# A two-lane decoder on one core: the halving inside silu moved into four weight tensors, and a new table for the order of the two lanes

## The chip, the core and the metric

The kernel runs on one core of a Trainium2 chip. The metric is the device time of one execution in microseconds (us), the median over several executions. The core has five instruction queues, each of which works in its own order: TensorE (PE, with its weight loads shown as PEld), VectorE (DVE), ScalarE (ACT), GpSimd (POOL) and SyncE (SP, which issues most transfers). Queues wait for each other through semaphores.

## What is computed

Four sequences of 512 rows by 128 columns pass through six sublayers, each followed by a layer norm. Only the fourth, a selective state-space recurrence, is touched by the change:

```python
x_and_res = x @ W_in
u, res = (x_and_res[..., :d_inner], x_and_res[..., d_inner:])
u = jax.nn.silu(u)
delta = jax.nn.softplus(u @ W_delta + b_delta)
Bm = u @ W_B
Cm = u @ W_C
def step(h, inp):
    d_t, B_t, C_t, u_t = inp
    dA = jnp.exp(d_t[..., None] * A)
    h = dA * h + d_t[..., None] * B_t[:, None, :] * u_t[..., None]
    y_t = jnp.einsum('bdn,bn->bd', h, C_t)
    return (h, y_t)
y = jnp.swapaxes(ys, 0, 1) + u * D_param
y = y * jax.nn.silu(res)
return y @ W_out
```

Ahead of it come a gated long convolution (hyena), a cross attention of one head (cross0) and a feed-forward layer with quantised weights (bitffn). Behind it come a cross attention of 16 heads (cross1) and a layer that weighs 1024 experts by product keys (experts).

## The kernel before

The kernel works on two sequences at a time, called lanes 0 and 1, in two passes: pass 0 does sequences 0 and 1, pass 1 does sequences 2 and 3. Everything of a lane lies in its own tiles (mem0, ps0, x0 and so on for lane 0, mem1, ps1, x1 for lane 1). Each engine's program is written once for a lane, as a generator that yields between pieces. A table of numbers, `LANE_RUNS`, has a row for each engine and says how many pieces of lane 0 to write into the queue, then how many of lane 1, and so on in turn. The order inside a lane is fixed. The table decides only how the two lanes lie between each other, but since each queue works in order, it decides who waits behind whom.

The recurrence (function `scan`) begins when DVE has written the lane's new x (L1472). PE transposes x (L712), ACT copies it (L1165), PE multiplies it by `m_in` (L866, four products of 128 x 512), and ACT takes the tanh of half of each (L1261). DVE forms (tanh + 1) times the product (L1637), which is twice silu. For the first two products, those of u, a second DVE step halves it into the tile `uu` (L1641). PE then needs both halves of `uu` for delta (L872, with `m_delta`), and for B and C (L878 and L884, with `m_bc`). ACT makes the softplus from absolute value, exponential and logarithm (L1268, L1273, L1276), and DVE adds it up (L1651, L1656) and multiplies by `uu` (L1659). Then 16 steps follow: ACT does the decay (L1291) and the input (L1310, in the first step L1299), PE transposes (L903), DVE scans (L1668), POOL multiplies by C (L1926), PE accumulates (L914). At the end DVE adds u times D (L1674) and gates with the other two products (L1678). Those last two keep their factor of two, which is taken out in L1678.

ACT has to load another function table (ACT_TABLE_LOAD) when the next function isn't in the loaded one. In the head of the recurrence tanh, the exponential and the logarithm alternate, so the order of the lanes sets how often.

In `experts` DVE weighs a tile of 128 x 1024 sums of key scores (L1844). Eight such tiles belong to a piece of 128 rows, and four pieces to a lane. The sums come from one of three engines: PE with a copy by ACT (L1087, L1165), DVE (L1827), or ACT (four groups of eight L1412). DVE also picks the best keys (L1778, L1799) and thresholds (L1802, L1804). In `cross1` a unit is eight ACT exponentials (L1368), behind two score matmuls (L1013) and a maximum by DVE (L1719, L1721).

Two semaphores matter: `p_late` is reached when the late weights, `m_delta`, `m_bc` and `m_D` among them, have been loaded, and `p_dve` counts steps of DVE in the preparation (4 of them before).

Of the kernel before, what the change touches and what calls it, by code (L numbers as in the profile page):

```python
# [72 lines left out]
def decoder(nc, x, ctx_1024, mask_BxSxS2_ik1, L0_attn_w_in, L0_attn_b_in, L0_attn_w_conv,  # L73
# [14 lines left out]
    DJ = DI // P  # L88
    NS = L1_attn_W_B.shape[1]
# [27 lines left out]
    with ExitStack() as ctx:  # L117
# [436 lines left out]
        for s in range(LANES):  # L554
            for k in range(NB):
# [10 lines left out]
            sync=("0 1 3 2 2 2 1 1 1 1 2 1 1 1 2 2 2 1 1 2 1 1 1 1 2 3 2 1 1 1 5 2 1 2 4 2 2 1 1 1 1 1 1 "  # L566
                "2 1 2 2 5 1 1 1"),
            tensor=("3 3 2 1 1 1 3 2 1 1 1 1 1 1 1 1 1 1 1 1 3 1 1 1 1 2 1 1 1 4 5 5 5 5 1 1 1 1 1 1 1 1 1 "
# [8 lines left out]
            scalar=("4 4 1 1 3 2 2 1 1 2 2 1 1 1 2 1 1 1 1 1 1 1 1 4 4 1 1 4 4 4 1 1 4 4 3 3 1 1 2 2 1 1 2 "  # L577
# [1411 lines left out]
```

## Time and profile before

| what | us |
|---|---|
| median of 3 runs (lowest 1017.96, highest 1019.2) | 1018.46 |
| the profiled execution: its time | 1017.51 |
| its span, first to last instruction | 1015.7 |
| PE busy in it | 776.3 |
| DVE busy | 759.6 |
| ACT busy | 686.5 |
| POOL busy | 317.7 |

No engine is busy for more than 76% of the span, so the sums by engine don't give the time. The kernel is a row of stages with other limits in each, and the time is read stage by stage: what an engine that is nearly always busy there has to do, and which waits it still has.

### The profile page before, as it was taken

What the parts mean: (1) busy time and instruction counts of PE and PEld (TensorE: products, weight loads), DVE (VectorE), ACT (ScalarE), POOL (GpSimd) and SP (SyncE); (2) the same over time, 40 slices, a digit from 0 to 9 for tenths busy, and PEclk for the clock granted to TensorE, in tenths of its full rate; (3) what the DMA queues carried; (4) which work ended last, traced back from release to release, by engine and by line L of the source; (5) the groups of instructions that cost most, each with busy time, mean ns of one, the idle gap of its engine ahead of it and who ended that gap; (6) DMA issues with size and microseconds to landing.
All of it is one profiled execution on the core that took longest, in us unless ns stands there. A gap on an engine that the chain in (4) does not pass through costs nothing.

```text
span 1015.7 us, 13734 instructions
## 1 busy us (share of the span) xinstructions
PE 776.3 (76%) x4486; PEld 568.2 (56%) x4488; DVE 759.6 (75%) x1635; ACT 686.5 (68%) x2061; POOL 317.7 (31%) x191
## 2 busy tenths in 40 slices
PE   1895586777978898797878468777797889889782
PEld 0584346666556555565657334666655744657561
DVE  2667857777655679999997875778766576998994
ACT  1445389995589489758534538999558859767850
POOL 3142107776466200000025210688746620000000
PEclk9987698999999899989987778799999999779997
DMA  6500012221000000010000000223100000000000
GB/s 163 157 1 1 0 47 70 87 93 43 21 1 1 1 1 1 1 37 1 1 22 1 0 1 29 86 88 95 45 19 1 1 1 0 1 1 1 1 1 21
DMA packets 28961, 29.04 MB, mean 29 GB/s; under 512 B 7268, under 2 KB 19290, under 8 KB 28890
## 3 DMA queue, kind: packets, MB, share of 16 engines
q1 hardware_dynamic: 26776, 27.19, 9.2%
q10 hardware_dynamic: 2114, 0.99, 0.4%
q8 instruction: 35, 0.57, 0.2%
q14 instruction: 36, 0.29, 0.1%
HBM read 26.33 MB, written 1.84 MB: 28 GB/s over the span
## 4 chain that ended last, share of the span: by engine, by line
DVE 36%; PE 26%; ACT 20%; POOL 7%; issue 5%; DMA 2%; POOLq 0%; DVEq 0%; ACTq 0%
DVE mem L1844 13%; ACT mem L1368 8%; DVE mem L1827 6%; POOL mem L1926 6%; ACT mem L1310 4%; ACT mem L1291 3%; PE ps L961 2%; PE ps L1134 2%; PE ps L1000 2%; PE ps L1098 2%; DVE mem L1668 2%; DVE mem L1778 2%; PE ps L1087 2%; PE ps L1036 1%; PE ps L1147 1%
## 5 line engine op out<-in xcount | busy, mean ns | idle before, releaser
L1884 POOL TENSOR_TENSOR rs<-ve,minus_half 128x4 f32<-128x4 f32 (+1 forms) x56 | 88.4, 1580 | 492.4 <-DVE ve L1465 419.6
L1926 POOL TENSOR_TENSOR mem<-mem 128x1024 f32<-128x1024 f32 x64 | 150.9, 2378 | 105.7 <-DVE mem L1668 103.6
L1668 DVE TENSOR_TENSOR_SCAN mem<-mem,ps 128x1024 f32<-128x1024 f32 x64 | 143.3, 2275 | 52.3 <-PE ps L903 52.0
L1844 DVE SCALAR_TENSOR_TENSOR mem<-mem 128x1024 f32<-128x1024 f32 x128 | 160.4, 1283 | 17.1 <-ACT mem L1165 10.4
L1412 ACT ACTIVATE mem<-mem 128x32 f32<-128x32 f32 x768 | 166.8, 313 | 7.1 <-PE ps L1134 7.1
L1134 PE MATMUL ps<-ident,mem 128*128 128x128 f32 x1024 | 140.8, 290 | 37.2 <-DVE mem L1844 35.2
L1165 ACT ACTIVATE mem<-ps 128x1024 f32<-128x1024 f32 (+6 forms) x127 | 92.9, 747 | 105.3 <-PE ps L1087 46.7
L1134 PEld LDWEIGHTS ps<-ident,mem 128*128 128x128 f32 x1024 | 120.4, 149 | 74.8 <-DVE mem L1844 52.3
L1368 ACT ACTIVATE mem<-ps,mem,rs 128x77 f32<-128x77 f32 x256 | 101.9, 449 | 21.2 <-DVE mem L1721 21.1
L903 PE MATMUL ps<-ident,mem 128*128 128x128 f32 x512 | 77.9, 307 | 47.9 <-ACT mem L1310 21.1
L1310 ACT ACTIVATE mem<-mem 128x256 f32<-128x256 f32 x240 | 100.2, 494 | 0.0
L903 PEld LDWEIGHTS ps<-ident,mem 128*128 128x128 f32 x512 | 65.0, 158 | 58.7 <-ACT mem L1310 43.5
L1087 PE MATMUL ps<-mem 64*128 64x512 f32 x160 | 83.2, 644 | 3.9 <-ACT mem L1165 3.3
L1291 ACT ACTIVATE mem<-mem,m_A 128x511 f32<-128x511 f32 x128 | 83.1, 708 | 3.3 <-DVE mem L1668 3.1
L1827 DVE TENSOR_TENSOR mem<-mem 128x1024 f32<-128x1024 f32 x64 | 77.6, 1223 | 0.1
L914 PE MATMUL ps<-ident,mem 128*128 128x128 f32 x512 | 68.6, 285 | 9.1 <-POOL mem L1926 8.9
L914 PEld LDWEIGHTS ps<-ident,mem 128*128 128x128 f32 x512 | 60.5, 148 | 14.3 <-POOL mem L1926 13.3
L1368 ACT ACTIVATION_READ_ACCUMULATOR mem<-ps,mem,rs 128x1 f32 x256 | 61.2, 239 | 0.0
L1940 POOL TENSOR_TENSOR mem<-mem 128x616 f32<-128x616 f32 x32 | 38.9, 1215 | 47.8 <-DVE mem L1740 47.8
L1013 PE MATMUL ps<-mem,xT 128*128 128x308 f32 x128 | 41.0, 444 | 12.9 <-ACT mem L1368 11.4
L1087 PEld LDWEIGHTS ps<-mem 64*128 64x128 f32 x160 | 28.3, 196 | 37.3 <-issue 31.1
L1036 PE MATMUL ps<-vw,mem 128*128 128x128 f32 (+1 forms) x320 | 45.2, 285 | 0.0
(228 smaller groups left out, 1283.4 us busy)
## 6 DMA issues: line engine op xcount, KB each, us to landing
mem<-bc_rows SPq DMA_DIRECT2D x64, 256.0 KB, 3.3
mem<-in_x_dram SPq DMA_DIRECT2D x4, 256.0 KB, 5.4
mem<-in_L_ffn_w_q_dram SPq DMA_DIRECT2D x2, 512.0 KB, 7.7
mem<-key_rows SPq DMA_DIRECT2D x2, 512.0 KB
out_dram<-x SPq DMA_DIRECT2D x4, 256.0 KB, 2.3
mem<-in_mask_BxSxS_ik_dram SPq DMA_DIRECT2D x4, 154.0 KB, 3.8
a_k<-in_L_xattn_Wk_dram SPq DMA_DIRECT2D x1, 512.0 KB, 7.6
key_rows<-mem SPq DMA_DIRECT2D x1, 512.0 KB, 8.3
```

What stands on the lines that cost most here:

```text
L903: mm = pe.transpose(ps[:, 2 + j, k * P:(k + 1) * P], DZ[s][:, n % 2, k, j * P:(j + 1) * P], ident[:])
L914: mm = pe.matmul(ps[:, k // 2, at:at + P], HC[s][:, (n - 1) % 2, j, k * P:(k + 1) * P], ident[:], start=(n == 1 and at == 0), stop=(n == N ...
L1087: mm = pe.matmul(ps[:, 2 + half, :], SIMT[s][rows, k % 2, h // 2, :], key_pick[rows, half * (NK // 2):(half + 1) * (NK // 2), :] .rearrang ...
L1134: mm = pe.matmul(ps[:, e // 4, (e % 4) * P:(e % 4 + 1) * P], WH[s][:, (k * PH + h) % WB, e * P:(e + 1) * P], ident[:], start=(h == 0 and e ...
L1291: ins = nc.scalar.activation(dA[s][:, n % 2, j, 1:S], DL[s][:, j, 1:S], ACT.Exp, scale=m_A[:, j, n:n + 1])
L1310: ins = nc.scalar.activation(DZ[s][:, n % 2, k, :], DUT[s][:, k, :], ACT.Identity, scale=BT[s][:, k, n:n + 1])
L1368: ins = nc.scalar.activation(SC[s][:, k % 2, h, :], ps[:, i // 4, i % 4 * C:(i % 4 + 1) * C], ACT.Exp, scale=RS[s][:, k * H + h:k * H + h ...
L1412: ins = nc.scalar.activation(WH[s][:, n % WB, i * NK:(i + 1) * NK], sims[:, 1, h, :], ACT.Identity, bias=sims[:, 0, h, i:i + 1])
L1668: nc.vector.tensor_tensor_scan((HS, TU)[n % 2][s][:].rearrange(flat), dA[s][:, n % 2].rearrange(flat), dbu.rearrange(flat), 0.0, ALU.mult, ...
L1827: summed[n] = own(nc.vector.tensor_tensor(WH[s][:, n % WB, :].rearrange("p (i j) -> p i j", i=NK), spread(views(k)[:, 0, h, :], 2, NK), sp ...
L1844: nc.vector.scalar_tensor_tensor(out=wh, in0=wh, scalar=TH[s][:, k % 2, h:h + 1], in1=wh, op0=ALU.is_ge, op1=ALU.mult).then_inc(G("wh_read ...
L1926: nc.gpsimd.tensor_tensor(HC[s][:, n % 2], (HS, TU)[n % 2][s][:], spread(CQ[s][:, n % 2, :], 1, DJ), ALU.mult)\
```

## The change

The step L1641 goes away: DVE writes (tanh + 1) times the product straight into `uu`, which now holds twice u. Whoever reads `uu` gets a factor that is taken out of the weights, once, in the first pass: `m_delta` times 0.5, the C part of `m_bc` times 0.5, `m_D` times 0.5, and the B part of `m_bc` times 0.25, since B multiplies delta times u and both hold the factor. These four steps stand on DVE at the start of lane 0's `bitffn` in pass 0. PE ahead of L872 and DVE ahead of L1674 now wait for the fifth step of `p_dve`. All five rows of the table are new.

```diff
         LANE_RUNS = dict(
-            sync=("0 1 3 2 2 2 1 1 1 1 2 1 1 1 2 2 2 1 1 2 1 1 1 1 2 3 2 1 1 1 5 2 1 2 4 2 2 1 1 1 1 1 1 "
+            sync=("1 1 5 2 1 2 2 2 1 1 1 1 1 1 2 2 1 1 1 1 2 2 1 3 2 1 1 1 5 2 1 2 2 1 3 1 1 1 1 1 2 2 1 "
...
                     w.next(G("silu_u", s), DJ)
+                    pe.wait_ge(p_dve, 5)
                     for m in range(DJ):
...
                     dve.wait_ge(p_late, ALL_LATE)
+                    if s == 0 and b == 0:
+                        yield 0
+                        nc.vector.tensor_scalar(m_delta[:], m_delta[:], 0.5, None, ALU.mult)
+                        nc.vector.tensor_scalar(m_bc[:, :, 0:NS], m_bc[:, :, 0:NS], 0.25, None, ALU.mult)
+                        nc.vector.tensor_scalar(m_bc[:, :, NS:2 * NS], m_bc[:, :, NS:2 * NS], 0.5, None, ALU.mult)
+                        nc.vector.tensor_scalar(m_D[:], m_D[:], 0.5, None, ALU.mult).then_inc(p_dve, 1)
                     yield 0
                     x_squares(s)
...
-                        ins = nc.vector.scalar_tensor_tensor(out=t[:, j % DJ, :], in0=t[:, j % DJ, :], scalar=1.0,
-                                                             in1=ps[:, at, :], op0=ALU.add, op1=ALU.mult)
-                        if j < DJ:
-                            w.link(ins)
-                            nc.vector.tensor_scalar(UU[s][:, j, :], t[:, j, :], 0.5, None, ALU.mult)\
-                                .then_inc(G("silu_u", s), 1)
-                        else:
-                            ins.then_inc(G("silu_r", s), 1)
+                        to = (UU if j < DJ else TR)[s][:, j % DJ, :]
+                        nc.vector.scalar_tensor_tensor(out=to, in0=t[:, j % DJ, :], scalar=1.0, in1=ps[:, at, :],
+                                                       op0=ALU.add, op1=ALU.mult)\
+                            .then_inc(G("silu_u" if j < DJ else "silu_r", s), 1)
...
                     w.next(G("y_acc", s), NS + 1)
+                    dve.wait_ge(p_dve, 5)
                     for j in range(DJ):
```

What the new table moves is shown at three places. In the changed kernel most lines stand one or two off: its L1643 is L1637 of before, L1616, L1618 and L1624 are L1611, L1613 and L1619 (the quantising and the last sum of `bitffn`), L1471 is L1472, L1260 is L1261, L1272 and L1275 are L1273 and L1276, L1846 and L1829 are L1844 and L1827, L1780 to L1806 are L1778 to L1804.

First, DVE where the recurrence starts in pass 0. Before:

```order
L1472 TENSOR_SCALAR x0<-r0,mv0,rs0 128x128 x4
L1472 TENSOR_SCALAR x1<-r1,mv1,rs1 128x128 x4
L1637 SCALAR_TENSOR_TENSOR mem0<-mem0,ps0 128x512
L1641 TENSOR_SCALAR mem0<-mem0 128x512
L1637 SCALAR_TENSOR_TENSOR mem0<-mem0,ps0 128x512
L1641 TENSOR_SCALAR mem0<-mem0 128x512
L1637 SCALAR_TENSOR_TENSOR mem0<-mem0,ps0 128x512 x2
L1637 SCALAR_TENSOR_TENSOR mem1<-mem1,ps1 128x512
```

The same place on DVE in the changed kernel:

```order
L1471 TENSOR_SCALAR x0<-r0,mv0,rs0 128x128 x4
L1616 TENSOR_SCALAR mem1<-mem1,rs1,st1 128x512
L1618 TENSOR_SCALAR mem1<-mem1 128x512
L1643 SCALAR_TENSOR_TENSOR mem0<-mem0,ps0 128x512 x4
L1624 SCALAR_TENSOR_TENSOR r1<-ps1,st1,r1 128x128 x4
L1458 BN_STATS bns1<-r1 128x6 x4
L1461 BN_AGGR mv1<-bns1 128x2 x4
L1464 TENSOR_SCALAR ve1<-mv1 128x4
L1471 TENSOR_SCALAR x1<-r1,mv1,rs1 128x128 x4
L1652 TENSOR_SCALAR mem0<-ps0,m_bdelta 128x512 x2
```

Lane 1's last sum of `bitffn` (L1619 of before, L1624) and its new x, which stood ahead of lane 0's silu, now stand behind it.

Second, ACT at the same place in pass 0. Before:

```order
L1261 ACTIVATE mem0<-ps0 128x512 x4
L1261 ACTIVATE mem1<-ps1 128x512 x4
L1268 ACTIVATE mem0<-ps0,m_bdelta 128x512 x2
L1273 ACT_TABLE_LOAD
L1273 ACTIVATE mem0<-mem0 128x1024
L1268 ACTIVATE mem1<-ps1,m_bdelta 128x512 x2
L1273 ACTIVATE mem1<-mem1 128x1024
L1276 ACT_TABLE_LOAD
L1276 ACTIVATE mem0<-mem0 128x1024
L1276 ACTIVATE mem1<-mem1 128x1024
```

The same place on ACT in the changed kernel:

```order
L1260 ACTIVATE mem0<-ps0 128x512 x4
L1267 ACTIVATE mem0<-ps0,m_bdelta 128x512 x2
L1272 ACT_TABLE_LOAD
L1272 ACTIVATE mem0<-mem0 128x1024
L1164 ACTIVATE xT1<-ps1 128x512
L1275 ACT_TABLE_LOAD
L1275 ACTIVATE mem0<-mem0 128x1024
L1164 ACTIVATE mem0<-ps0 32x512
L1164 ACTIVATE mem0<-ps0 128x64
L1260 ACT_TABLE_LOAD
L1260 ACTIVATE mem1<-ps1 128x512
```

Lane 0's tanh, exponential and logarithm now come in one go with only lane 1's copy of x between them, and lane 1's come later, with table loads of their own. Over the whole queue there are 16 loads in the place of 14, both new ones here.

Third, DVE where `experts` of lane 1 starts in pass 1. Before:

```order
L1844 SCALAR_TENSOR_TENSOR mem0<-mem0 128x1024
L1827 TENSOR_TENSOR mem0<-mem0 128x1024
L1844 SCALAR_TENSOR_TENSOR mem0<-mem0 128x1024
L1778 MAX mem1<-mem1 128x8 x16
L1790 TENSOR_TENSOR mem1<-mem1 128x8x8
L1790 TENSOR_TENSOR mem1<-mem1 128x8x12
L1790 TENSOR_TENSOR mem1<-mem1 128x8x4
L1796 TENSOR_REDUCE mem1<-mem1 128x8
L1799 MAX mem1<-mem1 128x8 x8
L1802 SCALAR_TENSOR_TENSOR mem1<-mem1 128x8
L1804 TENSOR_SCALAR mem1<-mem1 128x8
L1844 SCALAR_TENSOR_TENSOR mem1<-mem1 128x1024
```

The same place on DVE in the changed kernel, from lane 1's last key step on:

```order
L1806 TENSOR_SCALAR mem1<-mem1 128x8
L1780 MAX mem0<-mem0 128x8 x8
L1846 SCALAR_TENSOR_TENSOR mem0<-mem0 128x1024
L1829 TENSOR_TENSOR mem0<-mem0 128x1024
L1780 MAX mem0<-mem0 128x8 x8
L1846 SCALAR_TENSOR_TENSOR mem0<-mem0 128x1024
L1846 SCALAR_TENSOR_TENSOR mem1<-mem1 128x1024
```

Lane 1's first weighing stood behind two weighings of lane 0 and directly behind its own thresholds. It now stands behind six of lane 0, two of which (with other work of lane 0) are between its thresholds and it.

On ACT, lane 0's eight gelus and its first own sums (four groups of eight L1412) now follow each other in both passes with one copy of lane 0 between them. Before, in pass 1, seven copies of lane 1 and three of its gelus were mixed in, and in pass 0 six copies and two gelus. At the end of `cross1` in pass 1, lane 1 has four units of exponentials behind lane 0's last, and had two. In pass 0 it has two in both.

## Rows read from the trace of the kernel before

**Rows 1.** Part 1 of the page: busy us (share of the span) xinstructions.

```profile
PE 776.3 (76%) x4486; PEld 568.2 (56%) x4488; DVE 759.6 (75%) x1635; ACT 686.5 (68%) x2061; POOL 317.7 (31%) x191
```

**Rows 2.** Windows: from:to, length, busy us (xinstructions) by engine, TensorE clock, DMA, GB/s.

```profile
120.00:150.00 30.00, 26.44 (x96) 14.03 (x96) 15.94 (x28) 21.07 (x32) 0.48 (x1) 0.92 0.08 25
...
337.70:516.00 178.30, 155.94 (x850) 106.85 (x851) 161.80 (x399) 125.03 (x453) 5.72 (x5) 0.95 0.02 6
817.00:1000.00 183.00, 157.43 (x834) 108.42 (x834) 161.72 (x399) 123.09 (x447) 5.61 (x5) 0.92 0.00 1
```

**Rows 3.** Timeline of DVE, start of both recurrences: start, duration, instruction, idle before.

```profile
116.71 1.13 DVE L1619 SCALAR_TENSOR_TENSOR r<-ps,st,r 128x128 f32<-128x128 f32 x4
...
119.27 1.11 DVE L1472 TENSOR_SCALAR x<-r,mv,rs 128x128 f32<-128x128 f32 x4
...
125.35 0.69 DVE L1637 SCALAR_TENSOR_TENSOR mem<-mem,ps 128x512 f32<-128x512 f32 x1 [3.65 <-ACT mem L1261]
126.08 0.43 DVE L1641 TENSOR_SCALAR mem<-mem 128x512 f32<-128x512 f32 x1
126.42 0.68 DVE L1637 SCALAR_TENSOR_TENSOR mem<-mem,ps 128x512 f32<-128x512 f32 x1
...
127.48 1.30 DVE L1637 SCALAR_TENSOR_TENSOR mem<-mem,ps 128x512 f32<-128x512 f32 x2
...
151.85 2.29 DVE L1668 TENSOR_TENSOR_SCAN mem<-mem,ps 128x1024 f32<-128x1024 f32 x1 [4.68 <-PE ps L903]
...
595.59 1.12 DVE L1472 TENSOR_SCALAR x<-r,mv,rs 128x128 f32<-128x128 f32 x4 [0.44 <-POOL rs L1884]
```

**Rows 4.** Timeline of all engines, head of the recurrence in pass 1.

```profile
605.07 3.70 PE L872 MATMUL ps<-mem,m_delta 128*128 128x512 f32 x8 [0.52 <-DVE mem L1641]
...
610.80 1.06 ACT L1273 ACTIVATE mem<-mem 128x1024 f32<-128x1024 f32 x1
...
616.44 3.70 PE L872 MATMUL ps<-mem,m_delta 128*128 128x512 f32 x8 [0.42 <-DVE mem L1641]
...
616.67 1.28 ACT L1276 ACT_TABLE_LOAD   x1
...
628.32 2.29 DVE L1668 TENSOR_TENSOR_SCAN mem<-mem,ps 128x1024 f32<-128x1024 f32 x1 [5.23 <-PE ps L903]
```

**Rows 5.** Timeline of PE, head of the recurrence in pass 0.

```profile
130.62 7.03 PE L872 MATMUL ps<-mem,m_delta 128*128 128x512 f32 x16
```

**Rows 6.** Timeline of DVE, start of bitffn in pass 0.

```profile
84.16 0.43 DVE L1592 TENSOR_SCALAR mem<-mem 128x512 bf16<-128x512 f32 x1
...
90.57 2.73 DVE L1599 SCALAR_TENSOR_TENSOR mem<-ps,st,b 128x512 f32<-128x512 f32 x4 [3.77 <-remote]
```

**Rows 7.** Timeline of DVE, start of experts in pass 0 and in pass 1.

```profile
363.63 0.17 DVE L1804 TENSOR_SCALAR mem<-mem 128x8 f32<-128x8 f32 x1
369.45 1.28 DVE L1844 SCALAR_TENSOR_TENSOR mem<-mem 128x1024 f32<-128x1024 f32 x1 [5.65 <-ACT mem L1412]
...
840.58 0.17 DVE L1804 TENSOR_SCALAR mem<-mem 128x8 f32<-128x8 f32 x1
848.80 1.28 DVE L1844 SCALAR_TENSOR_TENSOR mem<-mem 128x1024 f32<-128x1024 f32 x1 [8.05 <-ACT mem L1165]
```

**Rows 8.** Timeline of ACT, start of experts in pass 1.

```profile
827.95 1.28 ACT L1421 ACT_TABLE_LOAD   x1
...
848.61 1.79 ACT L1412 ACTIVATE mem<-mem 128x32 f32<-128x32 f32 x8
```

**Rows 9.** Timeline of ACT, a table load in pass 0.

```profile
139.57 1.28 ACT L1276 ACT_TABLE_LOAD   x1
140.87 2.00 ACT L1276 ACTIVATE mem<-mem 128x1024 f32<-128x1024 f32 x2
```

**Rows 10.** Timeline of ACT: lane 1's last unit of cross1 in pass 1.

```profile
813.55 0.42 ACT L1368 ACTIVATE mem<-ps,mem,rs 128x77 f32<-128x77 f32 x1 [3.38 <-DVE mem L1721]
```

**Rows 11.** The chain that ended last (start, length, what): two units without a gap.

```profile
786.70 6.54 ACT mem L1368 x32
```

More of the change, by code:

```diff
@@ L565, in decoder @@
         LANE_RUNS = dict(
-            sync=("0 1 3 2 2 2 1 1 1 1 2 1 1 1 2 2 2 1 1 2 1 1 1 1 2 3 2 1 1 1 5 2 1 2 4 2 2 1 1 1 1 1 1 "
-                "2 1 2 2 5 1 1 1"),
-            tensor=("3 3 2 1 1 1 3 2 1 1 1 1 1 1 1 1 1 1 1 1 3 1 1 1 1 2 1 1 1 4 5 5 5 5 1 1 1 1 1 1 1 1 1 "
[8 rows of a table removed]
-            scalar=("4 4 1 1 3 2 2 1 1 2 2 1 1 1 2 1 1 1 1 1 1 1 1 4 4 1 1 4 4 4 1 1 4 4 3 3 1 1 2 2 1 1 2 "
[6 rows of a table removed]
-            vector=("3 3 2 1 2 2 2 1 1 1 1 1 1 1 1 1 1 1 1 2 4 3 1 2 2 1 2 4 1 1 1 1 4 4 1 1 1 1 1 1 1 1 2 "
[8 rows of a table removed]
-            gpsimd=("1 1 3 3 2 1 2 3 1 1 1 1 1 1 1 1 2 1 1 1 2 2 2 1 1 2 1 1 1 1 2 1 1 2 1 2 2 2 1 1 3 2 2 "
-                "1 1 2 2 1 1 2 1 1 1 1 1 1 1 2 1 1 1 1 3 3 4 4 1 1 1 1 6 2 2 1 1 1 1 1 1 2 1 2 2 2 1 2 "
-                "1 3 3 2 2 1 1 2 2 1 1 2 2 1 1 2 1 1 1 1 1 1 1 3 1"))
+            sync=("1 1 5 2 1 2 2 2 1 1 1 1 1 1 2 2 1 1 1 1 2 2 1 3 2 1 1 1 5 2 1 2 2 1 3 1 1 1 1 1 2 2 1 "
+                "1 1 1 1 5 1 2 1"),
+            tensor=("2 1 1 2 4 1 1 2 1 2 1 1 1 1 1 1 1 2 2 1 2 1 2 3 1 1 1 1 2 2 4 5 5 3 1 1 1 1 2 2 2 2 4 "
[7 rows of a table added]
+            scalar=("2 1 2 3 3 3 2 1 1 1 1 2 2 1 1 1 1 1 2 2 1 1 1 1 1 1 1 1 4 3 1 1 1 1 2 3 1 1 7 1 3 1 2 "
[6 rows of a table added]
+            vector=("3 3 3 1 1 3 2 2 1 1 5 1 1 1 1 1 1 1 1 1 2 2 1 1 1 1 2 2 1 2 1 1 4 2 2 2 1 3 1 1 2 2 1 "
[7 rows of a table added]
+            gpsimd=("1 1 3 3 4 4 1 1 1 1 4 2 1 1 1 1 1 1 2 2 1 1 1 1 2 2 1 1 2 4 3 2 2 1 1 2 2 1 1 2 2 1 1 "
+                "2 1 1 1 1 2 3 2 2 3 3 4 4 1 1 1 1 4 1 3 1 1 1 1 1 2 2 1 1 1 1 2 1 1 4 1 1 1 1 1 1 3 2 "
+                "3 1 2 2 1 3 1 1 1 2 1 1 1 5 1"))
         def in_turn(program, lane_runs):
```

42 rows, old and new, of tables (scalar, tensor, vector) are left out of this document.

## The prediction, on record before the changed kernel ran

> **What bounds the kernel now.** First the page's busy times [rows 1]: the busiest engine, PE, works for 76% of the span and DVE for 75%. So no engine's total gives the time, and a microsecond taken from DVE's total gives a microsecond only where DVE is what everything waits for. Next I cut the span into stages and read which engine is busy there [rows 2]. At the start of the recurrence in pass 0, from 120 to 150 us, DVE works 15.9 of 30 us and ACT 21.1: neither is full, and what counts is the chain from x to the first scan. In `experts` DVE works 161.8 of 178.3 us in pass 0 and 161.7 of 183.0 in pass 1, more than 88% in both. There the stage is DVE's work plus DVE's idle time, 16.5 and 21.3 us. Then I went to those idle times on DVE's timeline [rows 7]: the longest of each stage is a single wait, 5.65 us in pass 0 and 8.05 us in pass 1. Both stand in front of an L1844 right behind a lane 1 threshold step, early in the stage.
>
> **The change part by part.**
>
> *The eight halving steps that go.* Two for each lane and pass make eight L1641. From one L1637 to the next it takes 1.07 us with the halving between (125.35 to 126.42), and two without it take 1.30, so 0.65 each [rows 3]. Each removal frees 1.07 - 0.65 = 0.42 us of DVE, 3.4 us in all. On the path to the end much less of it counts. In pass 0 both lanes' L872 run in one piece with no wait shown [rows 5]: PE was still busy with L866, and it hides the halving. In pass 1 PE waits for the halving 0.52 and 0.42 us [rows 4], together 0.94. I take 0.9 us as gain; the bounds are 0 and 3.4.
>
> *The four new steps.* The nearest row for the largest, `m_delta` with 128 x 512, is a step of the same kind and width at 0.43 us [rows 6]. The other three have 2 to 32 columns, so each costs less: 4 x 0.43 = 1.7 us is the upper bound, nothing the lower. Their cover is the wait behind them: lane 0's quantised x was done at 84.16 + 0.43 = 84.6 us, and DVE then stood still 3.77 us before L1599, on PE's side of the work [rows 6]. I take nothing. If the new order has removed that cover, it costs up to 1.7 us.
>
> *The two waits for the fifth step.* PE's stands in front of L872, which ran from 130.62 us [rows 5], while lane 0's `bitffn`, where the four steps stand, was past its first step at 84 us [rows 6]; DVE's stands behind all 16 scans. Both find it done. Behind PE's wait all of the recurrence's matmuls are queued, so only a late step would cost, and none is late. I take nothing.
>
> *The table, where the recurrence starts in pass 0.* Lane 1's block from 116.71 to 119.27 stood ahead of lane 0's x [rows 3]. It now stands behind it, so lane 0's x can start 2.6 us sooner, near 116.7. From there to the first scan: in pass 1, where lane 0 already went first, it took 628.32 - 595.59 = 32.7 us, but 616.67 - (610.80 + 1.06) = 4.8 of these passed between exponential and the load for the logarithm, with lane 1's four tanh in the queue [rows 3, 4]. Those four are gone from that place in pass 0, which leaves 27.9 us and a first scan at 116.7 + 27.9 = 144.6 where it was 151.85 [rows 3]: lane 0 gains 7.2 us. Lane 1 pays: DVE reaches its last sum only after waiting for lane 0's tanh (3.65 us idle in the same situation before) and after four L1637 of 0.65, together 6.3 us. Half of each lane, (6.3 - 7.2) / 2, is -0.5 us, and that I take, because a stage that both lanes share moves with their mean. The bounds are what one lane alone would give: 7.2 us gained, or 6.3 lost with the two new table loads on top.
>
> A load starts at 139.57 and the logarithm behind it at 140.87 [rows 9], so a switch takes 1.30 us and two take 2.6. I count them as covered by ACT's 8.9 idle us between 120 and 150 [rows 2]; without that cover they cost 2.6, and the upper bound is 6.3 + 2.6 = 8.9.
>
> The Trainium skill, "ScalarE: Activation LUTs", section "What ACT_TABLE_LOAD costs", speaks against the change: it puts a switch at about 2.66 us, the load of 1283 ns and a drain of 1380 ns behind it. By that rule the two would cost 5.3 us, and if none of it were covered the time would be near 1015 instead of near 1010. The trace disagrees: the load's 1.28 us is there, the drain is not, since the logarithm starts 1.30 us after the load [rows 9].
>
> *The table, where `experts` starts.* In pass 1 lane 1's first L1844 waited 8.05 us for its sums' copy by ACT [rows 7], with lane 0's weighings queued behind it. But lane 0 couldn't have gone on either: its own ACT sums ended at 848.61 + 1.79 = 850.4, which is 22.4 us after the table load at 827.95 [rows 8]. The new ACT queue does these sums without lane 1's copies between them, and the new DVE queue puts six weighings of lane 0, not two, ahead of lane 1's first. In pass 0 the wait of 5.65 us was for these same ACT sums. If both waits vanish, 13.7 us are gained. If what is late next is as late, nothing is: next come lane 1's copies and gelus, now behind lane 0's sums on ACT. I take half, 6.9 us, the middle of bounds that no row tells apart. DVE has work for that time, so the gain is one of the whole stage.
>
> *The sum.* -0.9 - 0.5 - 6.9 = -8.3 us. The profiled execution took 1017.51 us, of which its span is 1015.7, and gives 1009.2. The median of the runs shown is 0.95 us higher, so I predict 1018.46 - 8.3, rounded to **1010 us**.
>
> **The rivals.**
>
> *More.* Both waits vanish and lane 0's lead isn't paid for by lane 1: -0.9 - 7.2 - 13.7 = -21.8 us, 996.7. For it: DVE would be near full in both `experts`, and nothing but the order kept it idle. Against it: other idle time, 16.5 - 5.65 = 10.9 us in pass 0, is spread over waits that another order can lengthen.
>
> *No change.* The waits move on instead of closing, since each queue works in order and a piece put ahead waits itself: -0.9 - 0.5 = -1.4, 1017.1. For it: pass 1 had lane 0 ahead, pass 0 had the lanes level, and yet the two `experts` took 178.3 and 183.0 us, with the same DVE work, so the order is worth only some us.
>
> *Slower.* In pass 1 lane 1 now has four units of `cross1` behind lane 0's last, not two. With both lanes at work a unit takes 6.54 / 2 = 3.3 us [rows 11]. With lane 1 alone ACT stands still 3.38 us in front of a unit [rows 10], since the next scores wait for the last exponentials. Two more such units cost 2 x 3.38 = 6.8 us in which ACT does nothing, and lane 0's gelus, which need another table, are queued behind them. If that is not made up and the waits of `experts` are only moved, it is -0.9 + 6.8 = +5.9, or 1024.4. It decides as soon as lane 1's last four units show such gaps in front of each while lane 0's first L1844 hasn't started. Against it: lane 0 is ahead by just that much, and DVE can pick its best keys meanwhile.
>
> **How the numbers follow.** The forecast (1003 to 1016) has a chance of 0.48, the larger gain 0.14, no change 0.14, slower 0.24. A measurement of this kernel tells about 0.2% from no change, 2 us here. So faster by more than that (below 1016.4) has 0.62, within it 0.14, slower 0.24. The range runs from 998 to 1025. It takes in each term's bounds taken alone: with the full 13.7 us in `experts` the sum is -15.1, 1003.4; with the 8.9 us lost at the start of the recurrence it is +1.1, 1019.6; with nothing gained in `experts`, 1017.1. It also takes in most of the larger gain and most of the slower case, and leaves out about 0.08 below and 0.10 above.
>
> **What would show it.** Right: L1637's successors 0.65 us apart and no wait of L872 for them; the first scan of lane 0 near 145 us and of lane 1 later than before; no single DVE wait over 3 us in the first 40 us of either `experts`, and DVE idle there below 10 and 14 us. Wrong: a DVE wait of the same size at another L1844; `cross1` of pass 1 longer by more than 5 us with ACT gaps of some 3.4 us in front of lane 1's last units; or a granted clock in `experts` clearly under the 0.95 and 0.92 of before [rows 2], which would be a cost of the order that I have given no price.

## The result and the profile after

The changed kernel took 1030.65 us (median of 4 executions, 1027.21 to 1032.23) where the kernel before took 1018.21 on the same chip: 1.0119 of it, 95% interval 1.0099 to 1.0138. It is 12.4 us slower, outside the predicted range of 998 to 1025. The profiled execution took 1030.98 us with a span of 1029.2.

The page's busy times of the changed kernel answer to [rows 1].

```profile
PE 772.6 (75%) x4486; PEld 566.7 (55%) x4488; DVE 764.9 (74%) x1631; ACT 690.1 (67%) x2063; POOL 318.7 (31%) x191
```

They say little of the loss: DVE is busy 5.3 us longer (with four instructions fewer), ACT 3.6 and POOL 1.0, PE less. So I went by stages again. The next rows are windows of the changed kernel at the places of [rows 2]; both `experts` run from lane 0's x to lane 0's x.

```profile
120.00:150.00 30.00, 26.07 (x114) 13.74 (x113) 15.63 (x32) 24.90 (x40) 3.37 (x2) 0.94 0.09 29
331.70:520.30 188.60, 158.04 (x827) 109.31 (x827) 159.75 (x388) 127.25 (x454) 6.18 (x5) 0.91 0.02 6
824.30:1013.40 189.10, 157.16 (x871) 109.16 (x869) 165.66 (x406) 129.85 (x479) 8.03 (x8) 0.95 0.00 1
```

In pass 0 DVE works 159.75 of 188.6 us. Its idle time there is 28.9 us, and was 16.5 [rows 2]. These windows mix length and lag, since the lanes lie further apart now. So from here on a stage runs from the middle of the two lanes' new x (L1472 of before, L1471 here) to the next such middle. DVE's timeline of the changed kernel, the four rows around `experts` of pass 0:

```profile
331.67 1.37 DVE L1471 TENSOR_SCALAR x<-ps,mv,rs 128x128 f32<-128x128 f32 x4 [1.12 <-POOL rs L1886]
...
350.03 1.36 DVE L1471 TENSOR_SCALAR x<-ps,mv,rs 128x128 f32<-128x128 f32 x4 [1.12 <-POOL rs L1886]
...
520.29 1.12 DVE L1471 TENSOR_SCALAR x<-r,mv,rs 128x128 f32<-128x128 f32 x4 [0.90 <-POOL rs L1886]
...
530.02 1.12 DVE L1471 TENSOR_SCALAR x<-r,mv,rs 128x128 f32<-128x128 f32 x4 [1.13 <-POOL rs L1886]
```

The stage is (520.29 + 530.02)/2 - (331.67 + 350.03)/2 = 184.3 us, and the lanes enter it 18.4 us apart (their lag). All stages by the same reckoning, with two kernels of the experiments (one profiled execution each):

| stage, us | before | changed | fold alone | table alone |
|---|---|---|---|---|
| until the recurrence, pass 0 | 119.9 | 119.9 | 118.6 | 123.4 |
| recurrence | 137.8 | 137.8 | 139.9 | 138.4 |
| cross1 | 85.0 | 83.2 | 84.9 | 83.2 |
| experts | 176.2 | **184.3** | 175.5 | **180.2** |
| hyena, cross0, bitffn of pass 1 | 80.2 | **85.1** | 80.0 | **85.8** |
| recurrence | 141.3 | **142.9** | 139.7 | **146.2** |
| cross1 | 82.2 | **85.1** | 82.8 | **85.9** |
| experts | 177.9 | 175.8 | 175.1 | 175.7 |

The profiled execution of the fold alone is 2.2 us below its median (given below), so the stages differ by some 2 us more in all than the medians do.

So three places lost time: `experts` of pass 0, the front of pass 1, and recurrence with `cross1` in pass 1. I had put a term on the first (as a gain), none on the second, and only a rival on the third.

**Experts.** DVE's timeline of the changed kernel, its longer waits at the start of both `experts` (answers to [rows 7]), and where lane 1's key maxima stand now (365.57):

```profile
342.54 1.59 DVE L1780 MAX8 mem<-mem 128x8 f32<-128x32 f32 x16 [3.15 <-ACT mem L1164]
...
356.35 1.28 DVE L1846 SCALAR_TENSOR_TENSOR mem<-mem 128x1024 f32<-128x1024 f32 x1
...
363.19 1.28 DVE L1846 SCALAR_TENSOR_TENSOR mem<-mem 128x1024 f32<-128x1024 f32 x1 [5.55 <-ACT mem L1411]
...
365.57 1.59 DVE L1780 MAX8 mem<-mem 128x8 f32<-128x32 f32 x16
...
398.72 1.29 DVE L1846 SCALAR_TENSOR_TENSOR mem<-mem 128x1024 f32<-128x1024 f32 x1 [3.52 <-ACT mem L1164]
...
844.59 1.29 DVE L1846 SCALAR_TENSOR_TENSOR mem<-mem 128x1024 f32<-128x1024 f32 x1 [6.74 <-ACT mem L1164]
```

DVE's timeline of the kernel before in pass 0: lane 0's third weighing, then lane 1's key maxima, which stood ahead of the wait of 5.65 us:

```profile
357.39 1.28 DVE L1844 SCALAR_TENSOR_TENSOR mem<-mem 128x1024 f32<-128x1024 f32 x1
...
360.27 1.59 DVE L1778 MAX8 mem<-mem 128x8 f32<-128x32 f32 x16 [1.59 <-ACT mem L1165]
```

ACT's timeline of the changed kernel: in pass 0 lane 0's own sums and behind them the copy of lane 1's x, in pass 1 the table load ahead of lane 0's gelus:

```profile
355.79 1.79 ACT L1411 ACTIVATE mem<-mem 128x32 f32<-128x32 f32 x8
...
357.96 5.19 ACT L1411 ACTIVATE mem<-mem 128x32 f32<-128x32 f32 x24
...
363.06 0.67 ACT L1164 ACTIVATE xT<-ps,p_norm 128x512 f32<-128x512 f32 x1
...
838.98 1.28 ACT L1420 ACT_TABLE_LOAD   x1
```

ACT does what I had read from its order: the sums stand together and end at 357.96 + 5.19 = 363.15, six us sooner than before (DVE's weighing that needs them began at 369.45 [rows 7], and begins at 363.19 now). But DVE also comes six us sooner, at 363.19 - 5.55 = 357.64 where it came at 369.45 - 5.65 = 363.80. One us of that is lane 0's third weighing, which ended at 358.67 and ends at 357.63. The other five are lane 1's key steps (360.27 to 363.80 before, with the wait of 1.59 us ahead of them): they filled that time, and now stand behind the weighing, from 365.57 on. They couldn't have filled it any more, because ACT's copy of lane 1's x now stands behind the same sums and starts at 363.06. So the wait stayed as long as it was. And new ones came: 3.15 us ahead of lane 0's key maxima, 3.52 us for a copy that ACT has queued behind lane 1's sums.

In pass 1 the wait of 8.05 us, of lane 1's first weighing for its copy, is gone. The 6.74 us at 844.59 are another wait: lane 0's first weighing waits for lane 0's first copy. ACT does lane 1's last unit of `cross1` ahead of lane 0's gelus and loads their table 838.98 - 824.34 = 14.6 us after lane 0's x, where it took 827.95 - 817.0 = 11.0 before [rows 2, 8].

**Recurrence and cross1 of pass 1.** DVE's timeline of the changed kernel at the end of lane 1's recurrence:

```profile
743.17 1.22 DVE L1710 TENSOR_REDUCE ve<-mem 128x16 f32<-128x1024 f32 x1 [2.15 <-ACT mem L1355]
...
748.14 2.29 DVE L1669 TENSOR_TENSOR_SCAN mem<-mem,ps 128x1024 f32<-128x1024 f32 x1
...
757.15 0.20 DVE L1742 RECIPROCAL mem<-mem 128x8 f32<-128x8 f32 x1 [3.36 <-ACT mem L1367]
759.63 0.80 DVE L1721 TENSOR_REDUCE mem<-ps 128x8 f32<-128x616 f32 x1 [2.27 <-PE ps L1012]
...
761.34 1.41 DVE L1676 SCALAR_TENSOR_TENSOR mem<-mem,m_D,ps 128x512 f32<-128x512 f32 x2 [0.71 <-PE ps L922]
...
770.57 1.12 DVE L1471 TENSOR_SCALAR x<-r,mv,rs 128x128 f32<-128x128 f32 x4 [0.21 <-POOL rs L1886]
```

Lane 1's last scan and its closing steps (L1676) stand behind `cross1` steps of lane 0 (L1710, L1742, L1721) that wait themselves. Lane 1's x comes 35.0 us after lane 0's (12.8 before), and then its last units of `cross1` run alone. ACT's timeline in front of three of lane 1's last five units (lane 0's last unit lies between the first and the second of these rows):

```profile
808.20 0.42 ACT L1367 ACTIVATE mem<-ps,mem,rs 128x77 f32<-128x77 f32 x1 [2.43 <-DVE mem L1723]
...
820.31 0.42 ACT L1367 ACTIVATE mem<-ps,mem,rs 128x77 f32<-128x77 f32 x1 [2.43 <-DVE mem L1723]
...
827.31 0.42 ACT L1367 ACTIVATE mem<-ps,mem,rs 128x77 f32<-128x77 f32 x1 [3.70 <-DVE mem L1723]
```

**The front of pass 1.** Two waits of PE in the changed kernel from 539.5 to 581 us (total, times, longest), which the kernel with the fold alone doesn't have in the same sublayer, `cross0`:

```profile
PE ps L736 <- DVE mem L1502: 5.2, 1, 5.2
PE ps L710 <- DVE x L1471: 4.5, 2, 4.2
```

By the middles of the lanes' new x, `cross0` took 28.6 us where it takes 24.6 with the fold alone; hyena lost 1.4 and `bitffn` none. That these two waits make the 4.0 us is argued from where they stand, not tested.

### The profile page after: what moved, and what is told of

Same layout as the page of the kernel before. It is cut to its first block, busy times and chain, and to the rows that moved or that the text cites. A ratio compares the mean times of both kernels' runs of the same rounds, so it can differ in the third digit from the quotient of the medians.

```text
span 1029.2 us, 13737 instructions
## 1 busy us (share of the span) xinstructions
PE 772.6 (75%) x4486; PEld 566.7 (55%) x4488; DVE 764.9 (74%) x1631; ACT 690.1 (67%) x2063; POOL 318.7 (31%) x191
## 4 chain that ended last, share of the span: by engine, by line
PE 26%; issue 23%; DVE 17%; ACT 16%; POOL 12%; DMA 2%; POOLq 0%; DVEq 0%; ACTq 0%
POOL mem L1928 8%; ACT mem L1367 4%; ACT mem L1411 4%; POOL rs L1886 3%; PE ps L1086 3%; DVE mem L1846 3%; DMA mem<-bc_rows 2%; ACT mem L1309 2%; PE ps L1133 2%; PE ps L960 2%; ACT mem L1290 2%; PE ps L1012 2%; PE ps L999 2%; DVE mem L1829 2%; DVE x L1471 2%
## 5 line engine op out<-in xcount | busy, mean ns | idle before, releaser
L1846 DVE SCALAR_TENSOR_TENSOR mem<-mem 128x1024 f32<-128x1024 f32 x128 | 160.5, 1278 | 23.3 <-ACT mem L1411 11.7
L1133 PEld LDWEIGHTS ps<-ident,mem 128*128 128x128 f32 x1024 | 119.7, 148 | 81.5 <-DVE mem L1846 57.0
L902 PEld LDWEIGHTS ps<-ident,mem 128*128 128x128 f32 x512 | 62.5, 153 | 51.6 <-ACT mem L1309 29.1
L1829 DVE TENSOR_TENSOR mem<-mem 128x1024 f32<-128x1024 f32 x64 | 77.4, 1218 | 0.0
L913 PEld LDWEIGHTS ps<-ident,mem 128*128 128x128 f32 x512 | 61.0, 149 | 26.2 <-POOL mem L1928 25.4
L1367 ACT ACTIVATION_READ_ACCUMULATOR mem<-ps,mem,rs 128x1 f32 x256 | 58.3, 228 | 0.0
L1012 PE MATMUL ps<-mem,xT 128*128 128x308 f32 x128 | 43.2, 463 | 13.6 <-ACT mem L1367 12.1
L1721 DVE TENSOR_REDUCE mem<-ps 128x8 f32<-128x616 f32 x32 | 25.6, 799 | 28.1 <-PE ps L1012 28.1
```

Source lines behind the costliest of these rows:

```text
L902: mm = pe.transpose(ps[:, 2 + j, k * P:(k + 1) * P], DZ[s][:, n % 2, k, j * P:(j + 1) * P], ident[:])
L913: mm = pe.matmul(ps[:, k // 2, at:at + P], HC[s][:, (n - 1) % 2, j, k * P:(k + 1) * P], ident[:], start=(n == 1 and at == 0), stop=(n == N ...
L1133: mm = pe.matmul(ps[:, e // 4, (e % 4) * P:(e % 4 + 1) * P], WH[s][:, (k * PH + h) % WB, e * P:(e + 1) * P], ident[:], start=(h == 0 and e ...
L1367: ins = nc.scalar.activation(SC[s][:, k % 2, h, :], ps[:, i // 4, i % 4 * C:(i % 4 + 1) * C], ACT.Exp, scale=RS[s][:, k * H + h:k * H + h ...
L1846: nc.vector.scalar_tensor_tensor(out=wh, in0=wh, scalar=TH[s][:, k % 2, h:h + 1], in1=wh, op0=ALU.is_ge, op1=ALU.mult).then_inc(G("wh_read ...
```

## The experiments

Sixteen kernels ran, each with the kernel before on the same chip. "Fold" is the change without its table. The two orders of a table pass, in each engine, through common states (as many pieces of lane 0 and of lane 1 done), so one can follow the one order up to such a state and the other behind it, and nothing else moves. The edits of the table are given in words below, since its rows are long. The cuts, as the number of pieces done by each engine:

```
cut                                    PE   ACT  DVE  POOL  SP
front: in bitffn, pass 0               62    57   46    18    4
scan:  mid recurrence, pass 0         108   122   82    37   26
X:     mid cross1, pass 0             166   164  125    64   38
E:     lane 1 leaves cross1           199   178  170    79   39
W:     lane 1's thresholds            209   190  194    80   39
P:     start of pass 1                325   294  308    87   41
R:     start of its recurrence        374   337  358   104   41
S:     mid recurrence, pass 1         399   380  380   116   58
```

### Fold or table

```diff
 fold_alone:   the changed kernel with
-LANE_RUNS of the change, a `yield 0` ahead of the four steps
+LANE_RUNS of before
 table_alone:  the kernel before with
-LANE_RUNS of before
+LANE_RUNS of the change, an empty piece where the four steps stand
```

> The fold with the order of before: the eight L1641 are gone, the four new steps stand at the same place on VectorE, and the lanes lie in all five queues as before. Theory T, the loss of 12.4 us comes from the new order: the fold alone gives what the prediction's first term says, 0 to 3.4 us gained, so 1015 to 1018.5. Rival F, the fold itself costs (a wait for the fifth step, or two lanes that meet in another phase because each is 0.84 us sooner): 1022 or more.

> The new order with the halving kept in both lanes and no step on the weights. Theory T: the whole loss is here, 1029 to 1033. Rival F: most of it is gone, 1018 to 1024. If the two together (this one and the fold alone, each against the kernel before) don't add up to 12.4 us, the fold and the order act on each other.

Fold alone 1015.83 us (before 1018.5; 0.997, 0.9955 to 0.9986). Table alone 1033.31 (1.0141, 1.0126 to 1.0155). -2.7 + 14.8 = 12.1 beside the 12.4 of both: they add, and all of the loss is the table's. F falls. (The table alone came out just above T's 1029 to 1033.)

### One stretch of the new order at a time

```diff
-LANE_RUNS: order of before throughout (with the fold)
+new_until_cross1:  new up to X
+new_in_head0:      new from front to scan
+new_front0:        new up to front
+new_until_scan0:   new up to scan
+new_in_cross1:     new from X to E
+new_from_weighing: new from W to P
+new_in_experts0:   new from X to P
+new_in_front1:     new from P to S
+new_in_end:        new from S on
```

> The fold, with the new order in all five queues until the middle of cross1 in pass 0 and the order of before from there on (the two orders pass through the same state at that point, so nothing else is moved). By the stage lengths of the changed kernel, stretch by stage (theory L, each stretch of the new order costs what its own stage shows): the recurrence and cross1 of pass 0 were 1.8 us shorter, so 1015 to 1018. Rival C, the lag between the lanes that the new order makes in the recurrence (18.4 us between the two new x of experts in place of 10.1) is carried on and costs the later stages: 1022 or more although all of them have the old order.

> The fold, with the new order only from the middle of cross1 in pass 0 to the end of experts in pass 0, and the order of before ahead of it and behind it. Theory L: experts of pass 0 was 8.1 us longer with the new order, so about 1017.5 + 8 = 1025 (1022 to 1028). Rival C, the lag made earlier is what costs: 1016 to 1020.

> The fold, with the new order only in the second half of cross1 in pass 0. Theory S (the loss is made by the order of sums and weighings inside experts): in the trace of the kernel with the new order in cross1 and experts, the mean of the two lanes' new x ahead of experts was 2.1 us later than with the fold alone, so at most that: 1015 to 1019. Rival G (the loss is made by the gap between the lanes, 17.7 us at experts in place of 9.7, which this half of cross1 makes): 1021 to 1027.

> The fold, with the new order only in the rest of experts of pass 0 (ScalarE from lane 0's first sums on, VectorE from lane 1's thresholds on), and the order of before ahead of it, so that the lanes enter experts as before. Theory S: experts was 8 us longer from x to x with the new order, so 1022 to 1026. Rival G: 1014 to 1018.

> The fold, with the new order only from the start of pass 1 to the middle of its recurrence. By the stage lengths of the changed kernel the front of pass 1 cost 4.8 us more, but its lanes came in 9.7 us apart in place of 6.1. If its own order makes the loss: 1019 to 1022. If the loss was brought in by experts: 1013 to 1017.

> The fold, with the new order only from the middle of the recurrence in pass 1 to the end. This holds lane 1's last four units of cross1 alone and the third place of the change (six weighings of lane 0 ahead of lane 1's first). By the stage lengths of the changed kernel it costs 4.4 us until experts and gives 2.0 back: 1016 to 1020. The prediction's own term (half of a wait of 8.05 us gained) would give 1010 to 1013, its slower rival (two units in the open, 6.8 us) 1020 to 1024.

> The fold, with the new order only from the end of bitffn in pass 0 to the middle of the recurrence, so the first two of the three places shown (lane 0's silu ahead of lane 1's new x, the two added table loads). The prediction's term is -0.5 beside the fold (bounds -7.2 and +8.9), so 1013 to 1017. Rival: the 3.7 us that the new order gains until cross1 come from here: 1010 to 1013. If the loads and lane 1's later start cost: 1018 or more.

> The fold, with the new order only in the front of pass 0 up to the middle of bitffn. If the 3.7 us gained until cross1 lie here: 1010 to 1013. If not: 1014 to 1018.

> The fold, with the new order until the middle of the recurrence of pass 0. Front and head together; if the gain is made where the two fit together (the head alone had lane 1 come 9.6 us later and gained nothing): 1010 to 1013. If it is made by cross1: 1015 to 1018.

| kernel | us | before | ratio, 95% |
|---|---|---|---|
| new_until_cross1 | 1012.10 | 1018.50 | 0.9935 (0.9922 to 0.9948) |
| new_in_experts0 | 1027.14 | 1018.50 | 1.0080 (1.0062 to 1.0098) |
| new_in_cross1 | 1018.63 | 1017.90 | 1.0017 (0.9992 to 1.0041) |
| new_from_weighing | 1028.75 | 1017.90 | 1.0112 (1.0093 to 1.0131) |
| new_in_front1 | 1028.71 | 1017.90 | 1.0099 (1.0074 to 1.0124) |
| new_in_end | 1024.13 | 1017.90 | 1.0066 (1.0041 to 1.0090) |
| new_in_head0 | 1017.78 | 1017.27 | 1.0002 (0.9976 to 1.0028) |
| new_front0 | 1013.62 | 1016.95 | 0.9984 (0.9954 to 1.0015) |
| new_until_scan0 | 1016.33 | 1016.95 | 0.9996 (0.9982 to 1.0010) |

The new order costs in `experts` of pass 0, in the front of pass 1 and at the end of pass 1, as the stages said, and not at the start of pass 0. The stages of all profiles but that of the last experiment agree: `experts` of pass 0 takes 175.5 to 177.8 us in the ten kernels that have the order of before there, and 180.2 to 185.4 in the seven that have the new one. For the front of pass 1 it is 78.8 to 82.6 in twelve and 85.0 to 88.9 in five, for the recurrence and `cross1` of pass 1 together 221.9 to 223.6 in the twelve with the order of before from S on and 225.4 to 232.1 in the five with the new one.

`new_in_experts0` came out as L had it (1022 to 1028). Whether the order inside `experts` or the lag makes that loss is less clear. `new_in_cross1` makes a lag of 13.3 us into `experts`, not the 17.7 of G, and lies in the range of S; but it costs 3.4 us beside the fold alone, and `experts` takes 177.8 us in its profile, which is its fastest execution, where the fold alone takes 175.5. So a lag of 13 us may itself cost a little, and none of these kernels has one of 18 us with the order of before behind it. `new_from_weighing` lost more than S had given, with a lag of 12.8. But its longest wait of DVE, ahead of lane 1's key maxima, is one that the changed kernel doesn't have: ahead of W these stand early on DVE as before, and behind W ACT copies for them only after lane 0's sums. From DVE's timeline of `new_from_weighing`:

```profile
373.03 1.58 DVE L1782 MAX8 mem<-mem 128x8 f32<-128x32 f32 x16 [9.06 <-ACT mem L1166]
```

So it shows that the order can cost this much at such a lag, and not that it costs the same in the same way in the changed kernel. G is out as the whole cause at 13 us of lag; how the loss is shared at 18 us stays open.

`new_in_end` holds the place from which I had hoped for a gain in `experts` of pass 1. It costs 6.2 us, 8.9 beside the fold alone, just past the slower rival's 1020 to 1024. In its profile the recurrence of pass 1 takes 145.9 us (139.7 with the fold alone), `cross1` 85.2 (82.8) and `experts` 177.1 (175.1), so most of it is lost in the recurrence and not at lane 1's units of `cross1`, where the rival had it.

But the three stretches don't add. One at a time they cost, beside the fold alone (-2.7), 8.6 + 2.7 = 11.3, 13.5 and 8.9 us, 33.7 in all, where the whole table costs 15.1. `new_in_front1` shows why it missed both of its ranges: its front took 88.9 us, where the same order took 85.1 behind its own forerunner, and `experts` of pass 1 took 181.6 with the order of before, at a lower granted clock (last section).

`new_until_cross1` is faster than the kernel before, the fold alone and the changed kernel, and below the ranges of L and C both, so C falls. `new_front0` (1013.62) and `new_in_head0` (1017.78) fell between their ranges, and `new_until_scan0` into the one that puts the gain into `cross1`. Part of it may be no gain of the order: the fold alone took 1013.17 and 1014.12 us in its two executions at the mean clock of these four (0.901 and 0.902), 1.5 us above them, where the medians differ by 3.7. So where it is made, and how large it is, stays open.

### The order of before put back, one stretch at a time

```diff
-LANE_RUNS: new order throughout (the changed kernel)
+undo_experts0: order of before from X to P
+undo_front1:   order of before from P to R
+undo_end1:     order of before from S on
+undo_pass1:    order of before from P on
```

> The changed kernel with the order of before put back only from the middle of cross1 to the end of experts in pass 0. If the stages' losses add (experts 8 us, and some 2 us of it through the lanes that leave it 9.7 us apart): 1019 to 1023. If the losses act on each other, so that one stretch of the old order in the new is as wrong as the reverse: 1027 or more.

> The changed kernel with the order of before put back only from the middle of the recurrence in pass 1 to the end. If the last scans of lane 1 queued behind lane 0's cross1, and its last units alone, cost what the stage shows (4.4 us, given back 2.0 in experts): 1023 to 1028. If that stretch costs nothing in the place it stands: 1029 to 1032.

> The changed kernel with the order of before put back only in the front of pass 1 (hyena, cross0, bitffn). If the front loses 4.8 us of its own and the seam costs nothing: 1025 to 1027. If the seam loses again what the front gave: 1028 to 1032.

> The changed kernel with the order of before put back in all of pass 1 (from the start of its hyena on). If the front and the recurrence of pass 1 lose time of their own (4.8 and 4.4 us by their stages): 1020 to 1025, near new_in_experts0 less the gain until cross1. If they only carry what experts of pass 0 has lost: 1028 to 1031.

They took 1027.65, 1028.33, 1026.14 and 1021.12 us: 10.4, 11.1, 9.2 and 4.2 more than the kernel before beside them (ratios 1.0110, 1.0111, 1.0081 and 1.0036, each within 0.003 or so), where the changed kernel had 12.4. So with the new order in pass 0 ahead of it, the order of before put back in all of pass 1 gives 8.2 of the 12.4 back; put back in its front alone it gives 3.2, from S on alone 1.3. `undo_front1` and `undo_pass1` came out in the ranges for a loss of these stretches' own, `undo_end1` just past its range. `undo_experts0` missed my expectation of adding stages: `experts` fell back to 176.0 us, but the front of pass 1, whose lanes now came 6.1 and not 9.7 us apart, grew from 85.1 to 88.6. Of the 8.3 us that its stage gave back, the seam (the place where the one order follows on the other) took 3.5 again, and up to 4.1 may have been the clock's (last section).

### The wait itself

The changed place in ScalarE's program (the groups' old places are left empty):

```diff
                             nc.scalar.activation(GT[s][:, e, :], ps[:, e % 2, :], ACT.Gelu).then_inc(G("g_sb", s), 1)
+                            if e < 4:
+                                sims = SIM[s][:, 0, :].rearrange("p (h a n) -> p a h n", a=2, h=PH)
+                                for i in range(e * NK // 4, (e + 1) * NK // 4):
+                                    ins = nc.scalar.activation(WH[s][:, 2 % WB, i * NK:(i + 1) * NK],
+                                                               sims[:, 1, 2, :], ACT.Identity,
+                                                               bias=sims[:, 0, 2, i:i + 1])
+                                if e == 3:
+                                    ins.then_inc(G("asum_ready", s), 1)
```

> The fold with the order of before, but in both lanes and passes ScalarE's four groups of eight sums for the third weighing are taken out of their places and put behind the first four gelus, one group each. This closes VectorE's first long wait (5.66 us in pass 0) from the side of the engine that is waited for, which is what the prediction hoped of the new order. Premise P (a wait closed in experts is a gain of the stage, half of it at least): 1009 to 1013. Rival M (the wait moves to the gelus or copies that are now later, and the stage is as long): 1014 to 1019.

It took 1026.42 us (before 1017.27; 1.0097, 1.0059 to 1.0136), 9.2 more than the kernel before where the fold alone took 2.7 less. DVE's timeline of this kernel, start of `experts` in pass 0 and, the last row, in pass 1:

```profile
356.48 1.28 DVE L1860 SCALAR_TENSOR_TENSOR mem<-mem 128x1024 f32<-128x1024 f32 x1 [4.52 <-ACT mem L1166]
...
363.21 1.59 DVE L1794 MAX8 mem<-mem 128x8 f32<-128x32 f32 x16 [2.99 <-ACT mem L1166]
...
376.36 1.28 DVE L1860 SCALAR_TENSOR_TENSOR mem<-mem 128x1024 f32<-128x1024 f32 x1 [5.08 <-ACT mem L1166]
...
856.75 1.28 DVE L1860 SCALAR_TENSOR_TENSOR mem<-mem 128x1024 f32<-128x1024 f32 x1 [9.23 <-ACT mem L1166]
```

DVE's timeline of the fold alone at the same place in pass 0:

```profile
355.45 1.28 DVE L1847 SCALAR_TENSOR_TENSOR mem<-mem 128x1024 f32<-128x1024 f32 x1 [1.26 <-ACT mem L1166]
...
360.79 1.59 DVE L1781 MAX8 mem<-mem 128x8 f32<-128x32 f32 x16 [1.59 <-ACT mem L1166]
...
369.98 1.28 DVE L1847 SCALAR_TENSOR_TENSOR mem<-mem 128x1024 f32<-128x1024 f32 x1 [5.66 <-ACT mem L1413]
```

The wait for ACT's sums is gone, and its place is taken by waits for ACT's copies (L1166), which now stand behind those sums: 4.52, 2.99 and 5.08, together 12.6 us, where the fold alone has 1.26 and 1.59 for two such copies and 5.66 for the sums, 8.5. Both `experts` are some 7 us longer (182.4 and 181.7, with the fold alone 175.5 and 175.1). That is 4.1 of the 7 us in pass 0. P falls for this way of closing the wait, and M had too little: the wait didn't only move, it grew.

## Why the prediction was wrong

**The step that failed is the term for `experts`, -6.9.** I took half of two waits. In pass 0 the wait was 5.65 and is 5.55 us, for the reason above: I compared when the sums would be ready, and not when DVE would come for them, with lane 1's key steps gone from in front of them. In pass 1 the wait of 8.05 us went, but one of 6.74 us came ahead of lane 0's first weighing, and the stage was no shorter than with the fold alone (175.8 and 175.1). The stage of pass 0 grew by 8.8 beside the fold alone, some 4 of it with the granted clock (last section). The middle "of bounds that no row tells apart" was no middle: below zero there was room too, which I had written off with "if what is late next is as late, nothing is" gained. The rival of no change had the better mechanism there, that the waits move on, and also took zero for the worst. What I had put forward for it was misread: the windows of 178.3 and 183.0 us run from lane 0's x to lane 0's x. By the middles the two stages took 176.2 and 177.9 us, and the lanes entered them 10.1 and 11.5 us apart, so they said nothing of what an order costs.

Two of the signs that I had named for being wrong are there: DVE waits of over 5 us at another weighing (6.74), and a granted clock in `experts` of pass 0 of 0.91, not 0.95. The third isn't: `cross1` of pass 1 is 2.9 us longer than before, and I had named 5.

**Not priced: the front of pass 1.** The table is new there as well, and I looked at three places only. It cost 5.1 us beside the fold alone.

**The slower rival had a fair size, and its mechanism in part.** It gave 6.8 us for lane 1's units alone. Recurrence and `cross1` of pass 1 lost 3.2 + 2.3 = 5.5 beside the fold alone, 3.2 of it already in the recurrence, at lane 1's last scan and the steps behind it, which I had not seen. Of lane 1's four units behind lane 0's last, ACT stood still in front of two, 2.43 and 3.70 us; in front of the last it had lane 0's copies to do. Its sum, 1024.4, fell short by the other two places.

**The fold, -0.9 predicted, -2.7 measured,** within the bounds of 0 and 3.4. PE's timeline of the changed kernel, L871 in pass 1, shows neither of the waits of [rows 4] (0.52 and 0.42):

```profile
616.67 3.60 PE L871 MATMUL ps<-mem,m_delta 128*128 128x512 f32 x8
...
627.36 3.63 PE L871 MATMUL ps<-mem,m_delta 128*128 128x512 f32 x8
```

**The four steps, nothing:** right. DVE's timeline of the changed kernel has them at 69.67 us, the next step starts 0.58 us later, and the cover of [rows 6] is still there behind them (4.29 us). In the head of the recurrence the same timeline goes on so:

```profile
69.67 0.43 DVE L1582 TENSOR_SCALAR m_delta<-m_delta 128x512 f32<-128x512 f32 x1
...
70.25 0.15 DVE L1560 TENSOR_TENSOR st<-mv,rs 128x4 f32<-128x4 f32 x1
...
83.62 0.75 DVE L1604 SCALAR_TENSOR_TENSOR mem<-ps,st,b 128x512 f32<-128x512 f32 x1 [4.29 <-remote]
...
113.12 1.11 DVE L1471 TENSOR_SCALAR x<-r,mv,rs 128x128 f32<-128x128 f32 x4
...
120.58 0.69 DVE L1643 SCALAR_TENSOR_TENSOR mem<-mem,ps 128x512 f32<-128x512 f32 x1 [0.94 <-ACT mem L1260]
121.43 0.69 DVE L1643 SCALAR_TENSOR_TENSOR mem<-mem,ps 128x512 f32<-128x512 f32 x1 [0.17 <-ACT mem L1260]
...
139.82 2.28 DVE L1669 TENSOR_TENSOR_SCAN mem<-mem,ps 128x1024 f32<-128x1024 f32 x1
```

**The start of the recurrence, -0.5.** From x to first scan lane 0 takes 139.82 - 113.12 = 26.7 us, and I had worked out 27.9; that its scan came at 139.82 and not near 144.6 is for the most part its x, which came 3.6 us sooner than I had it. Lane 1 pays more than my 6.3: in `new_in_head0` its x stands 131.28 - 49.41 = 81.9 us behind lane 0's first x, with the fold alone 119.24 - 46.92 = 72.3. Both lanes' end of the recurrence, reckoned the same way, is only 1.0 us later there (212.5 against 211.6), so lead and lag nearly cancel. The intervals of the two kernels meet, and the term is settled no closer. One detail was wrong: L1643 follow each other at 0.85 us (120.58, 121.43), not 0.65, since ACT's tanh sets their pace. The added table loads cost what the trace of before said; ACT's timeline:

```profile
133.74 1.28 ACT L1260 ACT_TABLE_LOAD   x1
135.03 0.60 ACT L1260 ACTIVATE mem<-ps 128x512 f32<-128x512 f32 x1
```

A switch is 135.03 - 133.74 = 1.29 us. The Trainium skill, "ScalarE: Activation LUTs", section "What ACT_TABLE_LOAD costs", has about 2.66 us, load and drain; the measurement decides.

## What to carry to other kernels

A wait that an order should close has two ends: work out when the supplier is done and when the consumer now comes, since the order that brings the one forward can also take away the work that stood in front of the other. A new order is priced in every stage that it touches, with the lag between the lanes at each stage's start; the front of pass 1, which I had not looked at, cost 5 us here. And a stretch of an order is good or bad only behind the stretch ahead of it: putting back the order of a stage that had lost 8 us gave 2.

## What the hardware showed beside this

**The granted clock differs between executions of the same queues, and costs up to 6 us at one place.** In `experts` of pass 0 `undo_pass1` and `undo_end1` have the same queues from the start of the program on, and some 70 us into the stage the same times. Then the first was granted 0.93 and the second 0.58 for ten us. Windows of `undo_pass1`:

```profile
413.00:423.00 10.00, 9.39 (x47) 5.87 (x46) 9.86 (x27) 10.00 (x41) 0.00 (x0) 0.93 0.14 37
...
332.70:517.20 184.50, 152.36 (x827) 104.30 (x827) 159.62 (x387) 126.75 (x454) 6.18 (x5) 0.94 0.02 6
```

Windows of `undo_end1`, the same two stretches of its execution:

```profile
412.30:422.30 10.00, 10.00 (x31) 6.30 (x30) 9.54 (x28) 7.82 (x32) 0.00 (x0) 0.58 0.12 32
...
332.30:520.90 188.60, 158.06 (x827) 109.30 (x827) 159.70 (x388) 127.24 (x454) 6.18 (x5) 0.91 0.02 6
```

188.6 - 184.5 = 4.1 us with the same DVE work. The changed kernel's own profile has the same fall (184.3 us), and so has `undo_front1` (184.0); the table alone, like `undo_pass1`, doesn't (180.2). So of the 8.8 us that `experts` lost in the profiled execution (184.3 against 175.5) 4.7 are the order's, by these two, and 4.1 go with the clock. The order alone can cost more: in `new_from_weighing` the stage took 185.4 us at a mean clock of 0.97. The plainest place is `experts` of pass 1 in `new_in_front1` and `new_until_cross1`, again with the same queues there, though not ahead of it. Windows of the first:

```profile
916.10:926.10 10.00, 10.00 (x25) 5.11 (x24) 8.64 (x21) 1.26 (x2) 0.00 (x0) 0.50 0.00 0
```

and of the second, at the same distance from lane 0's x:

```profile
903.90:913.90 10.00, 8.54 (x56) 6.04 (x55) 9.88 (x26) 6.49 (x22) 0.00 (x0) 1.00 0.00 0
```

PE had been as busy in the ten us ahead of both (8.33 and 8.32 us, the clock 0.88 and 1.00 there). At 0.50, 1.2 GHz, four L1088 take 3.78 us where they take 1.98 at 2.4 GHz. These are PE's timelines, first of `new_in_front1`:

```profile
922.05 3.78 PE L1088 MATMUL ps<-mem 64*128 64x512 f32 x4
```

and of `new_until_cross1`:

```profile
906.42 1.98 PE L1088 MATMUL ps<-mem 64*128 64x512 f32 x4
```

What DVE then waited for PE in `new_in_front1` is on its timeline, a wait of 6.62 us that the other kernel doesn't have:

```profile
931.47 1.23 DVE L1817 TENSOR_TENSOR mem<-ps,mem 128x1024 f32<-128x1024 f32 x1 [6.62 <-PE ps L1135]
```

The spread of one kernel's executions goes with the clock: ten of `new_in_cross1` took from 1012.79 us at a mean clock of 0.904 to 1024.71 at 0.892. Since only one execution of each has a trace, that it is the cause of the spread isn't shown. What makes the clock fall in one execution and not in the other, the rows don't show; it stays open.
